# Feed-forward values in PSUM, offsets by two ScalarE passes, and GpSimd's scale products by position in the block

## The chip, the cores and the metric

The kernel runs on one core of one Trainium2 chip. The metric is the device time of one execution in microseconds (us); lower is better. The kernel before takes 913.84 us, the median of three runs (913.34 to 918.64).

Five engines work side by side, each with its own instruction stream: TensorE (PE), VectorE (DVE), ScalarE (ACT), GpSimd (POOL) and SyncE (SP, which here only issues DMAs). They wait for each other through semaphores. Each stream runs in the order in which it was written: an instruction whose semaphore isn't there yet holds up all that stand behind it on its engine.

## The reference

The input is x, 2 x 2048 rows of 128 values. Four residual steps follow each other: a landmark attention, a feed-forward, a linear attention, and the same feed-forward once more. The change touches the two feed-forward steps alone. In short:

```python
def fp4_quant_dequant(x):                      # blocks of 16 along the row
    scale = max(max|xb| / 6, 1e-12)
    xn = xb / scale
    idx = searchsorted(_MID, |xn|)             # nearest of 0 .5 1 1.5 2 3 4 6
    return _GRID[idx] * sign(xn) * scale

h = silu(q(x) @ q(w_gate).T) * (q(x) @ q(w_up).T)      # q is fp4_quant_dequant
y = q(h) @ q(w_down).T                                  # x: 128, h: 352 values a row
x = x + ffn(layernorm(x))
```

So each row's normalised x (128 values, 8 blocks) and each row's h (352 values, 22 blocks) is rounded to an eight-value grid with one scale for each block of 16.

## The kernel before, in words

The 4096 rows are 32 **tiles** of 128 rows (one row a partition). x is quantised by the **quad** (four tiles, 512 values a partition, q = 0 to 7), h by the **pair** (two tiles, 704 values a partition, r = 0 to 15). The function ffn(p) stands once in each engine's stream for each of the two feed-forward stages, p = 0 and p = 1.

**How a value is rounded.** DVE takes the largest magnitude of each block (absmax, L818). POOL makes the scale from it (L248), DVE its reciprocal (L823) and the ratio value/scale (ratio_of, L828). ACT writes an offset, the magnitude times 2^22, in bf16 (absolute, L557), DVE clamps that from below (offset_of, L834) and adds it to the ratio (move_by, L838). This addition rounds the ratio to its grid. POOL subtracts the offset again (L255 for x, L265 for h) and multiplies by the scales (L258, L268); there each scale is repeated 16 times by a step of zero. All of these tiles lie in SBUF.

**The rest of a pair.** PE transposes the four tiles of a quad (L1180), ACT copies them to SBUF (L534). For each tile PE makes gate and up (gate_up, L1188 and L1189) into two PSUM banks, ACT takes silu of the gate (L540), DVE multiplies it by up (gated, L845) into h. The rounded h is transposed by PE (L1197, six transposes a pair), copied by ACT (L546), multiplied by w_down on PE (L1206, twelve weight loads), copied by ACT (L552) and added to X by POOL (L273). In p = 0 DVE also takes statistics of finished tiles (L648, L650), and POOL makes the layernorm constants (L320). In p = 1 SP stores each finished quad (L234).

**The order.** Every engine's stream is a loop written out over r from -4 to 18, with q = (r + 4) // 2. Quads are worked on while q < 8, so up to r = 11: absmax, scale and ratio of a quad in the even iteration, the addition, POOL's passes, the transposes and the copy in the odd one. In iteration r:

- DVE: gated(2r), gated(2r+1), absmax of h, x part, reciprocal and ratio of h, x part, offset and addition of h.
- POOL: the scales of x (even r) and of pair r, the two passes of pair r-1, in odd r the two passes of quad q, the residual of pair r-3.
- PE: gate_up(2r+2), down of pair r-2, gate_up(2r+3), in odd r the transposes of quad q, the transposes of pair r-1.
- ACT: copy of pair r-2's transposes, silu(2r+2), down copy of pair r-2, silu(2r+3), offset of h for pair r, in even r that of x, in odd r normalise(q+1) (L526: four instructions, the layernorm of the next quad) and last the copy of quad q's transposes.

PSUM has eight banks. Banks 0 to 3 hold gate and up of two tiles, 4 and 5 the transposes of h, 6 those of x, 7 the down product. The functions that the change touches and what calls them:

## Time and profile before

| | |
|---|---|
| three runs, median | 913.84 us (913.34 to 918.64) |
| the profiled execution, its own time | 913.45 us |
| its span, first to last instruction | 911.7 us |
| mean granted TensorE clock | 0.85 |
| busy share: PE, PE weight loads | 70%, 51% |
| busy share: DVE, ACT, POOL | 64%, 33%, 39% |
| first feed-forward stage | about 383 to 547 us |
| second feed-forward stage | about 745 us to the end |

PE's row counts matmuls, PEld its weight loads, which overlap. A busy share is an average over stages with different limits, and idle time of an engine that is not the limit costs nothing; what bounds a stage is read from who waits for whom in it. The "chain of waits" follows the work back from its last instruction, at each step to what released it. The granted clock is the share of full speed that TensorE was given.

### The profile page before, as it was taken

The numbers are of one execution on the slowest core, as the hardware profiler recorded it, in microseconds if no ns is written. First come the engines' busy times: TensorE is split into PE (matmuls) and PEld (weight loads), VectorE is DVE, ScalarE is ACT, GpSimd is POOL, SyncE is SP. The second block draws the span as 40 slices with busy tenths as digits, with TensorE's granted clock in tenths as the row PEclk, the third lists the DMA queues.
The fourth block names the chain that finished last, engine by engine and source line by source line (L and its number), as shares of the span: only waits on it lengthen the run. The fifth ranks groups of instructions, "written<-read, shape, count | busy, mean of one in ns | idle before, by whom it ended". The sixth has DMA issues, their size and how long they took to land.

```text
span 911.7 us, 14036 instructions
## 1 busy us (share of the span) xinstructions
PE 639.3 (70%) x5231; PEld 464.9 (51%) x5231; DVE 584.0 (64%) x1062; ACT 300.4 (33%) x507; POOL 354.6 (39%) x423
## 2 busy tenths in 40 slices
...
DMA packets 13676, 10.47 MB, mean 11 GB/s; under 512 B 1399, under 2 KB 12599, under 8 KB 13493
## 3 DMA queue, kind: packets, MB, share of 16 engines
...
q14 instruction: 21, 0.16, 0.1%
...
## 4 chain that ended last, share of the span: by engine, by line
PE 48%; DVE 23%; POOL 13%; issue 10%; ACT 5%; ACTq 0%; DMA 0%; DVEq 0%; POOLq 0%
PE ps L1052 5%; PE ps L1138 4%; PE ps L1270 4%; PE ps L1206 3%; PE ps L1167 3%; PE ps L1079 3%; PE ps L1188 3%; POOL arena L268 3%; PE ps L1289 2%; POOL arena L265 2%; DVE r L770 2%; POOL arena L258 2%; PE ps L1197 2%; DVE arena L845 2%; DVE hblk L818 2%
## 5 line engine op out<-in xcount | busy, mean ns | idle before, releaser
L1188 PE MATMUL ps<-wguT,arena 128*128 128x352 f32 x128 | 61.9, 572 | 34.5 <-DVE arena L845 33.1
L320 POOL TENSOR_TENSOR ln<-mv,lnc 128x4 f32<-128x4 f32 x64 | 13.6, 213 | 154.7 <-DVE mv L650 154.7
L339 POOL MEMSET early<- 128x2560 f32 x2 | 4.5, 2231 | 172.3 <-PE ps L1123 161.6
L1138 PE MATMUL ps<-G,xw 128*126 128x512 f32 x72 | 46.6, 800 | 30.0 <-ACT xw L492 22.3
L1180 PE MATMUL ps<-eye,arena 128*128 128x128 f32 x64 | 15.3, 383 | 73.7 <-POOL arena L258 65.3
L368 POOL TENSOR_SCALAR_AFFINE_SELECT arena<-arena 128x1024 f32<-128x1024 f32 x32 | 35.0, 1093 | 80.6 <-ACT arena L607 80.6
L1206 PEld LDWEIGHTS ps<-wdT,arena 128*128 128x128 f32 (+1 forms) x384 | 57.7, 226 | 15.2 <-ACT arena L546 7.6
L1206 PE MATMUL ps<-wdT,arena 128*128 128x128 f32 (+1 forms) x384 | 58.4, 311 | 5.4 <-ACT arena L546 5.4
L268 POOL TENSOR_TENSOR arena<-arena,hblk 128x704 f32<-128x704 f32 x32 | 60.1, 1880 | 2.5
L1189 PE MATMUL ps<-wguT,arena 128*128 128x352 f32 x128 | 57.1, 532 | 0.0
L931 DVE TENSOR_TENSOR arena<-ps,tri 128x1024 f32<-128x1024 f32 x32 | 39.2, 1224 | 27.2 <-PE ps L1270 27.2
L828 DVE SCALAR_TENSOR_TENSOR arena<-arena,hblk 128x704 f32<-128x704 f32 x32 | 53.3, 1665 | 3.3
L1180 PEld LDWEIGHTS ps<-eye,arena 128*128 128x128 f32 x64 | 9.7, 186 | 82.3 <-POOL arena L258 64.2
L607 ACT ACTIVATE arena<-ps 128x1024 f32<-128x1024 f32 x32 | 32.8, 1025 | 53.7 <-PE ps L1270 53.7
L265 POOL TENSOR_TENSOR arena<-arena,hoff 128x704 f32<-128x704 f32 x32 | 48.6, 1519 | 4.1 <-PE ps L1197 1.6
L1188 PEld LDWEIGHTS ps<-wguT,arena 128*128 128x128 f32 x128 | 24.7, 233 | 42.1 <-issue 39.3
L1197 PE MATMUL ps<-eye,arena 128*128 128x128 f32 (+1 forms) x192 | 37.2, 348 | 12.2 <-POOL arena L268 12.2
L1148 PEld LDWEIGHTS ps<-band,A 126*32 126x32 f32 x1152 | 32.3, 122 | 24.4 <-DVE A L795 20.9
L1148 PE MATMUL ps<-band,A 126*32 126x114 f32 x1152 | 35.5, 287 | 13.0 <-DVE A L795 13.0
L540 ACT ACTIVATE arena<-ps 128x352 f32<-128x352 f32 x64 | 29.6, 463 | 43.1 <-PE ps L1188 42.9
L1052 PE MATMUL ps<-arena 128*128 128x128 f32 x288 | 37.4, 289 | 8.9 <-DVE arena L734 7.2
L770 DVE TENSOR_REDUCE r<-ps 126x48 f32<-126x1536 f32 x12 | 21.1, 1755 | 33.7 <-PE ps L1138 33.7
...
## 6 DMA issues: line engine op xcount, KB each, us to landing
...
```

What stands on the lines that cost most here:

```text
L265: tt(out=hgrid, in0=hmoved[k], in1=hoff[k][:, :], op=ALU.subtract).then_inc(s["fh_grid"], 1)
L268: tt(out=blocks(hquant[k].rearrange("p k n -> p (k n)")), in0=blocks(hgrid), in1=hblk[k][:, 2, :].unsqueeze(2).broadcast_to([P, 2 * F // B ...
L770: reduce(out=r1[:, 0, :], in_=psf[0:WI, 0:NW * HM].rearrange("p (k m) -> p k m", m=M), axis=AX, op=ALU.max).then_inc(s["s1_max"], 1)
L828: stt(out=rat.rearrange("p (k j) -> p k j", j=BLK), in0=src.rearrange("p (k j) -> p k j", j=BLK), scalar=TIE, in1=b[:, 1, :].unsqueeze(2). ...
L931: tt(out=masked[n % 2][:, 0:8, :], in0=psf[:, 0:2 * QW].rearrange("p (h t) -> p h t", t=P), in1=tri[:, :].unsqueeze(1).broadcast_to([P, 8, ...
L1052: last = mm(banks(bank + hf, 1, P)[:, u, :], lhsT[:, 4 * hf + u, :], rhs[:, 4 * hf + u, :], start=True, stop=True)
L1138: last = mm(ps[0:WI, w, :], xw[:, w * WO:w * WO + WI], G1[:, b, :], start=True, stop=True)
L1148: last = mm(ps[32 * c:32 * c + 32, 4 + g, w * WO:(w + 1) * WO], A1v[:, w, h * M:(h + 1) * M], band[:, h, :], start=True, stop=True)
L1188: mm(ps[:, 2 * k, 0:F], x, wguT[:, 0:F], start=True, stop=True).then_inc(s["f_gate"], 1)
L1189: mm(ps[:, 2 * k + 1, 0:F], x, wguT[:, F:2 * F], start=True, stop=True).then_inc(s["f_up"], 1)
L1197: last = tp(ps[0:FK[c], 4 + k, c * P:(c + 1) * P], hquant[r % 2][:, k, c * P:c * P + FK[c]], eye[:, :])
L1206: last = mm(ps[:, 7, k * P:(k + 1) * P], hT[r % 2][0:FK[c], k, c, :], wdT[0:FK[c], c, :], start=(c == 0), stop=(c == 2))
```

## The change

- The normalised x is written by ACT into PSUM bank 7; maximum, ratio (in place) and addition read it there. The gated product is written over the up values in PSUM (banks 1 and 2, or 3 and 4, by the pair's parity), and h's maximum, ratio (in place) and addition work there.
- All gates share bank 0. The transposes of x and of h's first tile share bank 5; those of h's second tile and the down product share bank 6. The waits follow from that.
- The offset is no longer Abs on ACT and a clamp on DVE, but Square on ACT, a wait, and Identity with a constant bias on ACT, both bf16.
- POOL's scale products walk by position in the block: for each of 16 positions all blocks in turn, so that in0 and the output step by 16 values (64 bytes) and the scales are read one after the other.
- The copy of h's transposes is two instructions, one a tile.
- On PE and ACT, the transposes of quad q and their copy now stand between the first and the second tile's gate/up and silu of an odd iteration. normalise(q+1) stays where it was, which is now behind that copy.
- In p = 1 DVE adds the down product to X straight from PSUM; ACT's down copy and POOL's residual are left out there. In p = 1 ACT waits for the end of the linear attention before normalise(0).

The core of the diff, without most of the removed lines, which the listing above has, and with indentation taken off; the parts are, in order, GpSimd, ScalarE, VectorE and TensorE:

```diff
+GATE_BANK, X_BANK, T_BANK = 0, 7, 5
+SQ = (RND / 6.0) ** 0.5
...
+def up_banks(r):
+    return ps[:, 1 + 2 * (r % 2):3 + 2 * (r % 2), 0:F]
+def columns(t):
+    return t.rearrange("p (k j) -> p j k", j=BLK)
...
-    tt(out=blocks(xquant.rearrange("p k c -> p (k c)")), in0=blocks(xgrid),
-       in1=xblk[:, 2, :].unsqueeze(2).broadcast_to([P, QD * P // BLK, BLK]), op=ALU.mult).then_inc(s["fx_quant"], 1)
+    tt(out=columns(xquant.rearrange("p k c -> p (k c)")), in0=columns(xgrid),
+       in1=xblk[:, 2, :].unsqueeze(1).broadcast_to([P, BLK, QD * P // BLK]), op=ALU.mult).then_inc(s["fx_quant"], 1)
...
-    tt(out=blocks(hquant[k].rearrange("p k n -> p (k n)")), in0=blocks(hgrid),
-       in1=hblk[k][:, 2, :].unsqueeze(2).broadcast_to([P, 2 * F // BLK, BLK]), op=ALU.mult).then_inc(s["fh_quant"], 1)
+    tt(out=columns(hquant[k].rearrange("p k n -> p (k n)")), in0=columns(hgrid),
+       in1=hblk[k][:, 2, :].unsqueeze(1).broadcast_to([P, BLK, 2 * F // BLK]), op=ALU.mult).then_inc(s["fh_quant"], 1)
...
-    if 0 <= r - 3 < PN:
+    if p == 0 and 0 <= r - 3 < PN:
         residual(r - 3)
...
     a.wait_ge(s["moment_step"], (p + p + 1) * TILES + (q + 1) * QD)
-    need(a, "fx_ratio", n)
+    need(a, "fx_moved", n)
...
-        last = act(xin[:, k * P:(k + 1) * P], X[:, t, :], ACT.Identity, scale=rstd[:, t:t + 1],
+        last = act(ps[:, X_BANK, k * P:(k + 1) * P], X[:, t, :], ACT.Identity, scale=rstd[:, t:t + 1],
...
+    act(xT[q % 2], ps[:, T_BANK, :].rearrange("p (k c) -> p k c", k=QD), ACT.Copy).then_inc(s["fx_T_copied"], 1)
+    act(sil[t % 2], ps[:, GATE_BANK, 0:F], ACT.Silu).then_inc(s["f_silu"], 1)
...
     need(a, "f_down", n - 1)
+    for k in range(2):
+        a.wait_ge(s["fh_T"], 2 * n + k + 1)
+        act(hT[r % 2][:, k, :, :], ps[:, T_BANK + k, 0:3 * P].rearrange("p (c n) -> p c n", c=3),
+            ACT.Copy).then_inc(s["fh_T_copied"], 1)
 def down_copy(r):
     n = ffn_pairs(p, r)
     a.wait_ge(s["f_down"], n + 1)
     need(a, "f_x_done", n - 1)
+    act(down[r % 2], ps[:, T_BANK + 1, 0:2 * P].rearrange("p (k c) -> p k c", k=2), ACT.Copy).then_inc(s["f_down_copied"], 1)
+def offset_x(q):
+    n = ffn_quads(p, q)
+    a.wait_ge(s["fx_ratio"], n + 1)
+    need(a, "fx_offset", n)
+    act(xsquare[:, :], ps[:, X_BANK, :], ACT.Square, scale=SQ).then_inc(s["fx_square"], 1)
+    a.wait_ge(s["fx_square"], n + 1)
+    need(a, "fx_grid", n)
+    act(xoff[:, :], xsquare[:, :], ACT.Identity, bias=lnc[:, 3:4]).then_inc(s["fx_offset"], 1)
+def offset_h(r):
+    n = ffn_pairs(p, r)
+    a.wait_ge(s["fh_ratio"], n + 1)
+    need(a, "fh_offset", n)
+    act(hsquare[:, :].rearrange("p (k n) -> p k n", k=2), up_banks(r), ACT.Square, scale=SQ).then_inc(s["fh_square"], 1)
+    a.wait_ge(s["fh_square"], n + 1)
+    need(a, "fh_grid", n - 1)
+    act(hoff[r % 2][:, :], hsquare[:, :], ACT.Identity, bias=lnc[:, 3:4]).then_inc(s["fh_offset"], 1)
+if p == 1:
+    a.wait_ge(s["lin_x_done"], TILES)
 normalise(0)
 for r in range(-FILL, PN + 3):
     q = (r + FILL) // 2
...
         hT_copy(r - 2)
     if 0 <= r + 1 < PN:
         silu(2 * r + 2)
-    if 0 <= r - 2 < PN:
+    if 0 <= r - 2 < PN and p == 0:
         down_copy(r - 2)
+    if r % 2 and q < QN:
+        xT_copy(q)
     if 0 <= r + 1 < PN:
         silu(2 * r + 3)
     if 0 <= r < PN:
-        absolute("fh", hratio, hoff[r % 2], ffn_pairs(p, r), ffn_pairs(p, r) - 1)
+        offset_h(r)
     if r % 2 == 0 and q < QN:
-        absolute("fx", xratio, xoff, ffn_quads(p, q), ffn_quads(p, q))
+        offset_x(q)
     if r % 2 and q + 1 < QN:
         normalise(q + 1)
-    if r % 2 and q < QN:
-        xT_copy(q)
...
+def x_blocks():
+    return ps[:, X_BANK:X_BANK + 1, :]
+def absmax_x(q):
+    n = ffn_quads(p, q)
+    v.wait_ge(s["fx_norm"], n + 1)
+    reduce(out=xblk[:, 0, :].unsqueeze(1), in_=blocks(x_blocks()), axis=AX, op=ALU.max,
+           apply_absolute_value=True).then_inc(s["fx_absmax"], 1)
+def ratio_x(q):
+    n = ffn_quads(p, q)
+    inverse("fx", xblk, n)
+    v.wait_ge(s["fx_inverse"], n + 1)
+    stt(out=blocks(x_blocks()), in0=blocks(x_blocks()), scalar=TIE,
+        in1=xblk[:, 1, :].unsqueeze(1).unsqueeze(3).broadcast_to([P, 1, QD * P // BLK, BLK]), op0=ALU.mult,
+        op1=ALU.mult).then_inc(s["fx_ratio"], 1)
+def move_x(q):
+    n = ffn_quads(p, q)
+    v.wait_ge(s["fx_offset"], n + 1)
+    need(v, "fx_grid", n)
+    tt(out=xmoved, in0=ps[:, X_BANK, :], in1=xoff[:, :], op=ALU.add).then_inc(s["fx_moved"], 1)
 def gated(t):
     n = ffn_tiles(p, t)
     v.wait_ge(s["f_silu"], n + 1)
     v.wait_ge(s["f_up"], n + 1)
+    up = up_banks(t // 2)[:, t % 2, :]
+    tt(out=up, in0=up, in1=sil[t % 2], op=ALU.mult).then_inc(s["f_h"], 1)
+def absmax_h(r):
+    v.wait_ge(s["f_h"], ffn_tiles(p, 2 * r + 2))
+    reduce(out=pair(hblk[r % 2][:, 0, :]), in_=blocks(up_banks(r)), axis=AX, op=ALU.max,
+           apply_absolute_value=True).then_inc(s["fh_absmax"], 1)
+def ratio_h(r):
+    n = ffn_pairs(p, r)
+    v.wait_ge(s["fh_inverse"], n + 1)
+    stt(out=blocks(up_banks(r)), in0=blocks(up_banks(r)), scalar=TIE,
+        in1=pair(hblk[r % 2][:, 1, :]).unsqueeze(3).broadcast_to([P, 2, F // BLK, BLK]), op0=ALU.mult,
+        op1=ALU.mult).then_inc(s["fh_ratio"], 1)
+def move_h(r):
+    n = ffn_pairs(p, r)
+    v.wait_ge(s["fh_offset"], n + 1)
+    need(v, "fh_grid", n - 1)
+    tt(out=pair(hmoved[r % 2]), in0=up_banks(r), in1=pair(hoff[r % 2][:, :]), op=ALU.add).then_inc(s["fh_moved"], 1)
+def residual(r):
+    v.wait_ge(s["f_down"], ffn_pairs(p, r + 1))
+    tt(out=X[:, 2 * r:2 * r + 2, :], in0=ps[:, T_BANK + 1, 0:2 * P].rearrange("p (k c) -> p k c", k=2),
+       in1=X[:, 2 * r:2 * r + 2, :], op=ALU.add).then_inc(s["f_x_done"], 1)
+for r in range(-FILL, PN + (4 if p == 0 else 3)):
     q = (r + FILL) // 2
+    if 0 <= r < PN:
         gated(2 * r)
         gated(2 * r + 1)
+        absmax_h(r)
+    if r % 2 == 0 and q < QN:
+        absmax_x(q)
+    if r % 2 and q < QN:
+        move_x(q)
+    if p == 1 and 0 <= r - 2 < PN:
+        residual(r - 2)
+    if 0 <= r < PN:
+        inverse("fh", hblk[r % 2], ffn_pairs(p, r))
+        ratio_h(r)
+    if r % 2 == 0 and q < QN:
+        ratio_x(q)
     if p == 0 and 0 <= r - 4 < PN:
         v.wait_ge(s["f_x_done"], ffn_pairs(p, r - 3))
         tile_stats(2, 2 * r - 8)
         tile_stats(2, 2 * r - 7)
+    if 0 <= r < PN:
+        move_h(r)
 ffn(0)
...
+def x_transposes(q, r):
     n = ffn_quads(p, q)
     pe.wait_ge(s["fx_quant"], n + 1)
+    need(pe, "fh_T_copied", 2 * ffn_pairs(p, min(max(r - 1, 0), PN)))
     for k in range(QD):
+        last = tp(ps[:, T_BANK, k * P:(k + 1) * P], xquant[:, k, :], eye[:, :])
     last.then_inc(s["fx_T"], 1)
 def gate_up(t):
+    n, r = ffn_tiles(p, t), t // 2
     pe.wait_ge(s["fx_T_copied"], ffn_quads(p, t // QD + 1))
+    need(pe, "f_silu", n)
     x = xT[t // QD % 2][:, t % QD, :]
+    mm(ps[:, GATE_BANK, 0:F], x, wguT[:, 0:F], start=True, stop=True).then_inc(s["f_gate"], 1)
+    need(pe, "fh_moved", ffn_pairs(p, max(r - 1, 0)))
+    mm(up_banks(r)[:, t % 2, :], x, wguT[:, F:2 * F], start=True, stop=True).then_inc(s["f_up"], 1)
 def h_transposes(r):
     n = ffn_pairs(p, r)
     pe.wait_ge(s["fh_quant"], n + 1)
+    need(pe, "fx_T_copied", ffn_quads(p, min((r + 1 + FILL + 1) // 2, QN)))
+    need(pe, "fh_T_copied", 2 * n)
+    for k in range(2):
+        if k == 1:
+            need(pe, "f_x_done" if p else "f_down_copied", n)
+        for c in range(3):
+            last = tp(ps[0:FK[c], T_BANK + k, c * P:(c + 1) * P], hquant[r % 2][:, k, c * P:c * P + FK[c]], eye[:, :])
+        last.then_inc(s["fh_T"], 1)
+def down_mms(r):
+    n = ffn_pairs(p, r)
+    pe.wait_ge(s["fh_T_copied"], 2 * n + 2)
     for k in range(2):
         for c in range(3):
+            last = mm(ps[:, T_BANK + 1, k * P:(k + 1) * P], hT[r % 2][0:FK[c], k, c, :], wdT[0:FK[c], c, :],
                       start=(c == 0), stop=(c == 2))
     last.then_inc(s["f_down"], 1)
...
         gate_up(2 * r + 2)
     if 0 <= r - 2 < PN:
         down_mms(r - 2)
+    if r % 2 and q < QN:
+        x_transposes(q, r)
     if 0 <= r + 1 < PN:
         gate_up(2 * r + 3)
-    if r % 2 and q < QN:
-        x_transposes(q)
     if 0 <= r - 1 < PN:
         h_transposes(r - 1)
```

## Rows read from the trace of the kernel before

**Rows 1.** Windows: length, busy us of PE, PEld, DVE, ACT, POOL (instructions), clock, DMA.
```profile
403.70:513.70 110.00, 70.93 (x324) 52.98 (x324) 94.65 (x148) 47.09 (x90) 78.82 (x79) 0.85 0.00 1
...
765.75:875.77 110.02, 70.85 (x324) 53.04 (x324) 90.08 (x112) 47.09 (x90) 72.37 (x63) 0.85 0.04 13
```

**Rows 2.** Chain of waits, second stage: start us, length us, what (xcount).
```profile
779.41 1.34 PE ps L1206 x12
...
784.72 0.90 DVE hblk L818
...
786.20 1.52 POOL arena L265
...
787.80 1.91 POOL arena L268
...
790.34 1.19 POOL arena L255
...
791.60 1.59 POOL arena L258
...
793.24 1.12 PE ps L1180 x4
...
795.64 1.17 PE ps L1188 x2
...
800.97 0.79 ACT hoff L557
```

**Rows 3.** Timeline of DVE: start us, us, engine, line, operation, output<-inputs, xcount.
```profile
782.93 0.89 DVE L838 TENSOR_TENSOR arena<-arena,hoff 128x704 f32<-128x704 f32 x1
...
783.74 0.94 DVE L845 TENSOR_TENSOR arena<-arena,ps 128x352 f32<-128x352 f32 x2
...
786.68 1.79 DVE L828 SCALAR_TENSOR_TENSOR arena<-arena,hblk 128x704 f32<-128x704 f32 x1
...
792.20 0.94 DVE L845 TENSOR_TENSOR arena<-arena,ps 128x352 f32<-128x352 f32 x2
...
795.60 0.43 DVE L823 RECIPROCAL hblk<-hblk 128x44 f32<-128x44 f32 x1 [0.95 <-POOL hblk L248]
```

**Rows 4.** Timeline of POOL beside an idle DVE, same columns.
```profile
389.52 1.06 POOL L258 TENSOR_TENSOR arena<-arena,xblk 128x512 f32<-128x512 f32 x1
...
900.43 1.38 POOL L268 TENSOR_TENSOR arena<-arena,hblk 128x704 f32<-128x704 f32 x1
```

**Rows 5.** Groups by line and shape: busy us, mean ns | idle before, releaser.
```profile
L540 ACT ACTIVATE arena<-ps 128x352 f32<-128x352 f32 x64 | 29.6, 463 | 43.1 <-PE ps L1188 42.9
...
L546 ACT ACTIVATE arena<-ps 128x768 f32<-128x768 f32 x32 | 25.8, 807 | 18.6 <-PE ps L1197 18.2
...
L534 ACT ACTIVATE arena<-ps 128x512 f32<-128x512 f32 x16 | 9.5, 595 | 50.2 <-PE ps L1180 50.2
...
L588 ACT ACTIVATE arena<-ps,bias_qk 128x512 f32<-128x512 f32 x8 | 5.5, 687 | 1.8 <-PE ps L1236 1.8
...
L363 POOL TENSOR_TENSOR arena<-arena 128x512 f32<-128x512 f32 x8 | 10.1, 1263 | 8.1 <-DVE arena L898 8.1
...
L885 DVE SCALAR_TENSOR_TENSOR arena<-ps,bias_qk,arena 128x512 f32<-128x512 f32 x8 | 6.0, 751 | 19.3 <-POOL arena L358 19.3
...
L770 DVE TENSOR_REDUCE r<-ps 126x48 f32<-126x1536 f32 x12 | 21.1, 1755 | 33.7 <-PE ps L1138 33.7
```

**Rows 6.** Timeline at the start and the end of the second stage.
```profile
747.17 0.33 POOL L248 TENSOR_SCALAR xblk<-xblk 128x32 f32<-128x32 f32 x1
...
749.26 1.63 ACT L526 ACTIVATE arena<-X,ln 128x128 f32<-128x128 f32 x4
...
875.77 0.94 DVE L845 TENSOR_TENSOR arena<-arena,ps 128x352 f32<-128x352 f32 x2
...
891.26 0.95 DVE L845 TENSOR_TENSOR arena<-arena,ps 128x352 f32<-128x352 f32 x2
...
908.26 0.72 POOL L273 TENSOR_TENSOR X<-X,arena 128x256 f32<-128x256 f32 x1 [4.38 <-ACT arena L552]
```

More of the change, by code:

```diff
@@ L81, in build @@
         ln = sb("ln", [P, 4, TILES])
-        lnc = sb("lnc", [P, 3])
+        lnc = sb("lnc", [P, 4])
         rstd, shift = ln[:, 1, :], ln[:, 3, :]
@@ L102, in build @@
         used[0] = 0
-        xin, xratio, xmoved, xgrid = (part(QD * P) for _ in range(4))
+        xmoved, xgrid = (part(QD * P) for _ in range(2))
         xquant = part(QD * P).rearrange("p (k c) -> p k c", k=QD)
@@ L106, in build @@
         sil = [part(F) for _ in range(2)]
-        h, hratio, hgrid = (part(2 * F) for _ in range(3))
+        hgrid = part(2 * F)
         hmoved = [part(2 * F) for _ in range(2)]
@@ L297, in _ @@
                 g.memset(XNT[:, b, HALO + N:NPAD], 0.0)
-            for k, c in enumerate((1e-5, -0.5, -1.0)):
+            for k, c in enumerate((1e-5, -0.5, -1.0, RND * 4.0 / 3.0)):
                 g.memset(lnc[:, k:k + 1], c)
@@ L533, in xT_copy @@
                     need(a, "f_up", ffn_tiles(p, (q - 1) * QD))
-                    act(xT[q % 2], ps[:, 6, :].rearrange("p (k c) -> p k c", k=QD), ACT.Copy).then_inc(s["fx_T_copied"], 1)
+                    act(xT[q % 2], ps[:, T_BANK, :].rearrange("p (k c) -> p k c", k=QD), ACT.Copy).then_inc(s["fx_T_copied"], 1)
                 def silu(t):
@@ L551, in down_copy @@
                     need(a, "f_x_done", n - 1)
-                    act(down[r % 2], ps[:, 7, 0:2 * P].rearrange("p (k c) -> p k c", k=2), ACT.Copy).then_inc(s["f_down_copied"], 1)
-                def absolute(name, rat, off, n, freed):
-                    a.wait_ge(s[name + "_ratio"], n + 1)
-                    need(a, name + "_grid", freed)
-                    act(off[:, :], rat, ACT.Abs, scale=RND).then_inc(s[name + "_abs"], 1)
+                    act(down[r % 2], ps[:, T_BANK + 1, 0:2 * P].rearrange("p (k c) -> p k c", k=2), ACT.Copy).then_inc(s["f_down_copied"], 1)
[17 more added lines that the diff above has]
+                    a.wait_ge(s["lin_x_done"], TILES)
                 normalise(0)
@@ L816, in ffn, with pair, blocks @@
             def ffn(p):
-                def absmax(name, src, b):
-                    reduce(out=b[:, 0, :], in_=src.rearrange("p (k j) -> p k j", j=BLK), axis=AX, op=ALU.max,
-                           apply_absolute_value=True).then_inc(s[name + "_absmax"], 1)
+                def pair(t):
+                    return t.rearrange("p (k n) -> p k n", k=2)
+                def blocks(t):
+                    return t.rearrange("p k (b j) -> p k b j", j=BLK)
                 def inverse(name, b, n):
@@ L823, in inverse @@
                     recip(out=b[:, 1, :], in_=b[:, 2, :]).then_inc(s[name + "_inverse"], 1)
-                def ratio_of(name, src, rat, b, n):
-                    v.wait_ge(s[name + "_inverse"], n + 1)
-                    nb = b.shape[2]
-                    stt(out=rat.rearrange("p (k j) -> p k j", j=BLK), in0=src.rearrange("p (k j) -> p k j", j=BLK), scalar=TIE,
-                        in1=b[:, 1, :].unsqueeze(2).broadcast_to([P, nb, BLK]), op0=ALU.mult,
-                        op1=ALU.mult).then_inc(s[name + "_ratio"], 1)
-                def offset_of(name, off, n):
-                    v.wait_ge(s[name + "_abs"], n + 1)
-                    ts(out=off[:, :], in0=off[:, :], scalar1=RND_MIN, scalar2=None, op0=ALU.max).then_inc(s[name + "_offset"], 1)
-                def move_by(name, rat, off, mov, n):
-                    v.wait_ge(s[name + "_offset"], n + 1)
-                    tt(out=mov, in0=rat, in1=off[:, :], op=ALU.add).then_inc(s[name + "_moved"], 1)
+                def x_blocks():
[17 more added lines that the diff above has]
+                    tt(out=xmoved, in0=ps[:, X_BANK, :], in1=xoff[:, :], op=ALU.add).then_inc(s["fx_moved"], 1)
                 def gated(t):
@@ L843, in gated @@
                     v.wait_ge(s["f_up"], n + 1)
-                    need(v, "fh_ratio", ffn_pairs(p, t // 2))
-                    tt(out=h[:, (t % 2) * F:(t % 2 + 1) * F], in0=sil[t % 2], in1=ps[:, 2 * (t % 2) + 1, 0:F],
-                       op=ALU.mult).then_inc(s["f_h"], 1)
-                for r in range(-FILL, PN + (4 if p == 0 else 0)):
+                    up = up_banks(t // 2)[:, t % 2, :]
[4 more added lines that the diff above has]
+                           apply_absolute_value=True).then_inc(s["fh_absmax"], 1)
@@ L852, in ffn @@
-                    if hh:
+                    if 0 <= r < PN:
                         gated(2 * r)
                         gated(2 * r + 1)
-                        v.wait_ge(s["f_h"], ffn_tiles(p, 2 * r + 2))
-                        absmax("fh", h, hblk[k])
-                    if x and k == 0:
-                        v.wait_ge(s["fx_norm"], nq + 1)
-                        absmax("fx", xin, xblk)
-                    if x and k == 1:
-                        offset_of("fx", xoff, nq)
+                        absmax_h(r)
@@ L865, in ffn @@
                         tile_stats(2, 2 * r - 7)
-                    if hh:
-                        inverse("fh", hblk[k], n)
-                        need(v, "fh_moved", n)
-                        ratio_of("fh", h, hratio, hblk[k], n)
-                    if x and k == 0:
-                        inverse("fx", xblk, nq)
-                        need(v, "fx_moved", nq)
-                        ratio_of("fx", xin, xratio, xblk, nq)
-                    if x and k == 1:
-                        move_by("fx", xratio, xoff, xmoved, nq)
-                    if hh:
-                        offset_of("fh", hoff[k], n)
-                        move_by("fh", hratio, hoff[k], hmoved[k], n)
+                    if 0 <= r < PN:
+                        move_h(r)
             ffn(0)
```

23 lines of the change are left out of this document (1 added, 22 removed).

## The prediction

> **What bounds the kernel now.** I read the windows first, then the chain of waits, then the timeline. The change lies in the two feed-forward stages alone. In each, the twelve row pairs from r = 1 to 12, in which new rows are still being quantised beside the pairs, take 110.0 us, 18.34 us per odd and even iteration, with DVE busy 82 to 86% [rows 1]. The chain of one such round [rows 2] shows what the page's sum does not: it starts with DVE's maximum in an odd iteration, goes through four POOL passes in a row (L265, L268, L255, L258), the x transposes, a gate/up, a down product and another gate/up, and comes back to DVE through ACT's L557 in the even iteration. DVE is nearly as full, so both matter.
>
> DVE's fullness is partly waiting. The ratio L828 takes 1.79 us when POOL is at work, the add L838 0.89 when it is not [rows 3], for the same 704 elements. L268 takes 1.91 us in the chain [rows 2] and 1.38 at 900.43, L258 1.59 against 1.06 at 389.52 [rows 4], DVE being idle there. In the timeline a stretched DVE pass ends about one plain duration after POOL's pass ends, so the two engines take turns. The gated product, one operand in PSUM, is not stretched: two take 0.94 us [rows 3].
>
> **The change, part by part.** Time 0 is the start of the gated products of an odd iteration, 783.74 in the trace. Handoffs are those of the rows: 0.04 us, 0.07 between POOL passes; DVE's next product starts 0.81 after its last add (782.93 to 783.74) [rows 3].
>
> *Removed.* Every DVE pass with two SBUF streams goes to PSUM, so I take the turns as gone: POOL 1.38 and 1.06 as in [rows 4], DVE unstretched. DVE's clamp (0.3 us) and, in the second stage, ACT's down copy and POOL's residual go; DVE does that residual. From L770 (1536 elements, 1.755) and the maximum (704, 0.90) [rows 2, 5] DVE takes 1.04 ns an element over 0.16 us, so 0.42 for 256.
>
> *Added on ACT.* One Abs (0.79, L557 [rows 2]) becomes Square, a wait on it, then Identity. L534 (512, 595 ns) and L546 (768, 807 ns) give 0.755 for 704 from PSUM. Identity is 0.79 plus a pointer bias: L588 against L534 prices it 0.09 [rows 5]. With 0.08 for the wait, the pair is 1.71, for x 1.39 (0.60, 0.08, 0.71). ACT wide over a wait has no nearer row; bounds 1.6 to 1.9.
>
> *POOL's scale products* (in0 and output now step 64 bytes, in1 is contiguous). At 512 elements the trace has 1.06 with a repeated in1 [rows 4], 1.19 with a bf16 in1 [rows 2], 1.26 with a contiguous fp32 in1 (L363 [rows 5]): 0.2 us for four more bytes an element. If a stepped fp32 read costs like twice its bytes, that is 0.2 once more: 1.47 for x, and for h 1.38 + 2 x 0.28 = 1.94. Bounds: no effect (1.06 and 1.38), and writes paying too (1.67 and 2.22). I take the middle, since both the new in1 and the new step are seen or implied by those rows.
>
> The Trainium skill (GPSIMD Engine Reference, section Performance pitfalls for Q7 kernels) speaks against this edit: a read stepping more than 8 bytes costs 2.9 cycles an element instead of 1.9. As an estimate, one cycle more at its 1.2 GHz makes 1.49 and 1.97, and the sum would be 1 us higher; no row shows a stepped read.
>
> *Moved: the order on PE and ACT.* This decides. In an odd iteration r, PE now transposes quad q before gate/up of tile 2r+3, and ACT copies it before silu of 2r+3; behind that silu stand the two offset passes of pair r, for which DVE's last add of the same iteration waits. But POOL gives quad q only after pair r's maximum, its scales, and both passes of pair r-1. So POOL's four passes are now inside DVE's own iteration, where before the transposes stood behind that gate/up and ACT's copy stood last. What this adds queues up everything behind: the add, the next products, POOL's next pass.
>
> Odd iteration: POOL's L265 starts at 2.46 [rows 2, 3] and ends 3.98; L268 4.05 to 5.99; L255 6.06 to 7.25; L258 7.32 to 8.79. Transposes 8.85 to 9.97 (1.12), gate half 1.17 to 11.15 [rows 2], PE being slow after a pause of over 5 us; silu 0.46 (L540 [rows 5]) to 11.65; offset to 13.41; the add and handoff 0.85: 14.26, against 8.46 before.
>
> Even iteration: the reciprocal starts 3.40 after the first product (792.20 to 795.60), the ratio 0.53 later [rows 3] (from POOL's scales, unchanged): 18.19, ends 19.14 with 0.95 as in the next paragraph. Offset 20.90, add 21.75. In the second stage ACT's normalise (1.60) runs to 15.0, the split hT copy 0.95 to 15.95, down 1.5 (1.34 in [rows 2], slower at times) to 17.5, DVE's new residual to 17.95, so the ratio is 0.35 later: 22.1. Mean round 21.9. Six are 131.5; r = 12 has no x work, -1.25. Against 110.0: +20.2 per stage.
>
> DVE on PSUM: the stt L885 with a PSUM input takes 0.751 us for 512, 0.06 over the 0.69 of 1.04 ns an element; L770, a reduce from PSUM, fits the same line as an SBUF one [rows 5]. I charge 0.06 on the ratio alone. The Trainium skill (VectorE: DVE Perf Modes, section The TRN2 errata) has a fixed 120 cycles for a PSUM source against 58 for SBUF; as an estimate, six passes on the path a round would then pay 0.065 each and the sum would be 4 us higher. Half the rows agree. Writes of DVE into PSUM are in no row: bounded by 0 and 0.3 us a round, taken as 0.
>
> Start of each stage, from POOL's scale at 747.17 [rows 6]: X's single bank makes normalise(1) wait for the first add, and ACT's new order puts it behind xT_copy(0), so behind POOL's first two passes. Scale, reciprocal and ratio to 748.75; offset 750.18; add 750.91; POOL 753.68; transposes and copy 755.48; normalise (1.63 [rows 6]) 757.1; maximum, scale, ratio 759.55; offset and add 761.7; POOL 764.5; transposes, gate/up(1) 768.0; product, maxima, scales, ratio 772.5; offset and add 775.1, where 765.75 stood: +9.3. ACT waiting for the end of the attention costs nothing, as POOL's moments end later still.
>
> Pairs 13 and 14 took 15.5 us (875.77 to 891.26 [rows 6]); without turns the recurrence (product and maximum 1.88, scales 0.54, reciprocal 0.53, ratio 0.95, offset 1.75, add 0.85, residual part 0.3) is 6.8, call it 7.0 for a slow PE: -1.5. The drain saves the down copy and most of POOL's 0.72 [rows 6] in the second stage: -1.1; -0.4 in the first.
>
> Sum: 2 x (9.3 + 20.2 - 1.5) - 1.5 = +54.5. The profiled execution took 913.45 us (span 911.7), 0.4 under the median 913.84. **Forecast 968 us.**
>
> **Rivals.**
> *A, faster.* The turns between DVE and POOL set the round, and the new order is covered. Then the round is DVE's own: even 3.40 + 0.53 + 0.95 + 1.76 + 0.85 = 7.49; odd 1.88 + 0.69 (x add) + 0.42 + 0.53 + 0.95 + 1.75 + 0.85 = 7.07. Of 18.34, 14.56 stay, and 12 x 3.78 = 45 us go: 868. For it: DVE at 82 to 86%. Against: the chain runs through POOL. It decides at the first odd iteration: only if the x transposes were ready before silu(2r+3) would ask, at about 3.2 us, while POOL's four passes alone end at 8.8. Chance 4%.
> *B, the step is free for POOL* (1.38 and 1.06): 0.97 a round and as much at the start: 968 - 13 = 955. Chance 20%.
> *C, writes pay too* (2.22, 1.67): +0.48 a round, +1 at the starts: 975. 13%.
> *D, the slow clock reaches further.* With PE pausing over 5 us a round, down and gate/up in the even iteration run at 1.2 GHz too: +1.2 a round, 982. For it: mean clock 0.85 now with shorter pauses [rows 1]. 13%.
> *E, PSUM operands don't end the turns*, so the change doesn't do what it says: POOL pays 0.53 twice in the odd iteration: 981. Against: the unstretched product. 4%.
> *F, partial hiding*: the starts cost half and PE is fast at once (-0.8 a round): 968 - 19 = 949; 10%. Something smaller still, within 1% of before: 3%.
> The forecast itself has 33%.
>
> **Numbers.** Range: B and F at the low end with part of each other, 944; D with the upper offset bound at the high end, 987. About 1% is what a measurement of this kernel tells from no change: slower by more than that 0.93 (all but A and the last), same 0.03, faster 0.04.
>
> **What would show it.** DVE idle for some 9 us (8 with the statistics of the first stage) in front of h's last add in odd iterations, and about 1 to 2 in even ones; rounds near 22 us; the transposes waiting for POOL and silu for them; POOL's h product at 1.9 and x at 1.5, never stretched; DVE's ratio at 0.95; DVE's share down, and the granted clock below 0.85. I am wrong if rounds are under 19 us, if DVE's add follows the ratio within 2 us in odd iterations, or if ratio passes still take 1.8.

## The result, and the profile after

The changed kernel takes 961.74 us, the median of four runs (960.36 to 966.51), against 914.25 us (913.34 to 918.64): 1.052 times the time before, 95% interval 1.048 to 1.056. The profiled execution took 962.55 us. I had forecast 968 us, 944 to 987.

The page of the changed kernel, and its windows over iterations 1 to 12 of both stages (columns as in [rows 1]):

```profile
span 960.8 us, 14051 instructions
...
PE 663.7 (69%) x5231; PEld 472.9 (49%) x5231; DVE 517.9 (54%) x1030; ACT 334.0 (35%) x571; POOL 343.2 (36%) x408
...
L899 DVE TENSOR_TENSOR arena<-ps,hoff 128x704 f32<-128x704 f32 x32 | 28.5, 892 | 111.7 <-ACT hoff L582 111.7
```

```profile
414.35:540.62 126.27, 76.81 (x318) 53.96 (x319) 65.30 (x130) 60.78 (x118) 75.20 (x75) 0.80 0.00 1
798.26:925.13 126.87, 78.88 (x318) 55.27 (x319) 62.68 (x106) 56.41 (x107) 64.17 (x53) 0.77 0.04 11
```

DVE fell from 584.0 to 517.9 us of work (64 to 54% of the span) while the kernel grew: its stretched passes and its clamps are gone. The granted clock fell from 0.85 to 0.84. L899, the last add of h, heads the list not for its work but for 111.7 us of waiting for ACT. The windows, which answer to [rows 1], took 110.0 and now take 126.3 and 126.9 us: 21.05 and 21.15 us a round against 18.34.

The chain of one round of the second stage (as [rows 2]) and DVE's timeline over it (as [rows 3]):

```profile
820.66 0.90 DVE hblk L885
822.15 1.52 POOL arena L275
...
825.70 1.18 POOL arena L265
826.94 1.53 POOL arena L268
828.51 1.11 PE ps L1230 x4
829.63 1.17 PE ps L1238 x2
...
832.77 1.51 ACT ps L536 x4
835.20 1.62 PE ps L1259 x12
837.64 0.91 DVE ps L891
839.36 0.89 ACT hoff L582
```

```profile
819.67 0.95 DVE L881 TENSOR_TENSOR ps<-ps,arena 128x352 f32<-128x352 f32 x2
...
823.67 0.90 DVE L891 SCALAR_TENSOR_TENSOR ps<-ps,hblk 128x704 f32<-128x704 f32 x1
832.90 0.89 DVE L899 TENSOR_TENSOR arena<-ps,hoff 128x704 f32<-128x704 f32 x1 [8.32 <-ACT hoff L582]
833.70 0.95 DVE L881 TENSOR_TENSOR ps<-ps,arena 128x352 f32<-128x352 f32 x2
...
840.27 0.89 DVE L899 TENSOR_TENSOR arena<-ps,hoff 128x704 f32<-128x704 f32 x1 [0.75 <-ACT hoff L582]
```

From 819.67 to 833.70 the odd iteration takes 14.03 us; the even one, which ends with the next product at 841.08, takes 7.38. The chain is the forecast one: DVE's maximum, POOL's L275 and L278 (2.02 us from 823.74, of which the chain shows most as a gap), L265, L268, the x transposes, the gate half, then ACT; normalise and down lead through DVE's residual (836.85, not shown) to the even iteration's ratio. DVE stands idle for 8.32 us in front of L899 in the odd iteration and 0.75 in the even one, and the ratio takes 0.90 us beside a busy POOL, where it took 1.79 [rows 3].

Groups by line that answer to [rows 5] and [rows 4], the start of the second stage (as [rows 6]), and its end:

```profile
L278 POOL TENSOR_TENSOR arena<-arena,hblk 128x704 f32<-128x704 f32 x32 | 65.0, 2032 | 2.5
...
L268 POOL TENSOR_TENSOR arena<-arena,xblk 128x512 f32<-128x512 f32 x16 | 24.3, 1519 | 1.3
...
L582 ACT ACTIVATE hoff<-hsquare,lnc 128x704 bf16<-128x704 bf16 x32 | 28.2, 882 | 1.0
...
L579 ACT ACTIVATE hsquare<-ps 128x704 bf16<-128x704 f32 x32 | 24.1, 755 | 16.4 <-DVE ps L891 16.4
...
L881 DVE TENSOR_TENSOR ps<-ps,arena 128x352 f32<-128x352 f32 x64 | 30.8, 524 | 11.8 <-PE ps L1240 9.7 <-ACT arena L550 2.2
L891 DVE SCALAR_TENSOR_TENSOR ps<-ps,hblk 128x704 f32<-128x704 f32 x32 | 28.8, 899 | 1.1
```

```profile
770.77 0.33 POOL L258 TENSOR_SCALAR xblk<-xblk 128x32 f32<-128x32 f32 x1 [0.18 <-DVE xblk L859]
...
778.89 1.60 ACT L536 ACTIVATE ps<-X,ln 128x128 f32<-128x128 f32 x4
```

```profile
940.38 0.95 DVE L881 TENSOR_TENSOR ps<-ps,arena 128x352 f32<-128x352 f32 x2
...
957.64 0.42 DVE L903 TENSOR_TENSOR X<-ps,X 128x256 f32<-128x256 f32 x1 [5.58 <-PE ps L1259]
```

POOL's products take 2.03 and 1.52 us where they took 1.38 and 1.06 undisturbed [rows 4]; Square and Identity 0.755 and 0.882; the gated product and the ratio write PSUM at 0.52 and 0.90 us, as they wrote SBUF. From POOL's scale at 770.77 to iteration 1 at 798.26 go 27.5 us, against 18.6 [rows 6]. After iteration 15's products (940.38) 20.4 us are left, against 20.4 from 891.26 [rows 6].

| stretch (profiled executions, us) | before | after | difference | forecast |
|---|---|---|---|---|
| up to the first stage's iteration 1 | 403.7 | 414.4 | +10.7 (1.7 of it ahead of the stage) | +9.3 |
| iterations 1 to 12, first stage | 110.1 | 126.3 | +16.2 | +20.2 |
| from 13 to the first scan of the attention | 45.6 | 42.1 | -3.5 | -1.9 |
| linear attention | 185.1 | 185.2 | +0.1 | 0 |
| start of the second stage | 21.3 | 30.3 | +9.0 | +9.3 |
| iterations 1 to 12, second stage | 110.0 | 126.9 | +16.9 | +20.2 |
| from 13 to the end | 35.9 | 35.7 | -0.3 | -2.6 |

### The profile page after: what moved, and what is told of

It reads as the page before. It is cut to its first block, busy times and chain, and to the rows that moved or that the text cites. A ratio compares the mean times of both kernels' runs of the same rounds, so it can differ in the third digit from the quotient of the medians.

```text
span 960.8 us, 14051 instructions
## 1 busy us (share of the span) xinstructions
PE 663.7 (69%) x5231; PEld 472.9 (49%) x5231; DVE 517.9 (54%) x1030; ACT 334.0 (35%) x571; POOL 343.2 (36%) x408
## 4 chain that ended last, share of the span: by engine, by line
PE 42%; DVE 23%; POOL 12%; issue 12%; ACT 9%; POOLq 0%; ACTq 0%; DMA 0%; DVEq 0%
PE ps L1102 5%; PE ps L1188 4%; PE ps L1322 4%; PE ps L1217 3%; PE ps L1129 3%; POOL arena L275 3%; POOL arena L268 2%; PE ps L1341 2%; DVE ps L881 2%; DVE hblk L885 2%; DVE r L796 2%; ACT hoff L582 2%; PE ps L1259 2%; POOL arena L265 2%; ACT hsquare L579 2%
## 5 line engine op out<-in xcount | busy, mean ns | idle before, releaser
L899 DVE TENSOR_TENSOR arena<-ps,hoff 128x704 f32<-128x704 f32 x32 | 28.5, 892 | 111.7 <-ACT hoff L582 111.7
L1251 PE MATMUL ps<-eye,arena 128*128 128x128 f32 (+1 forms) x192 | 40.1, 367 | 46.2 <-POOL arena L278 46.2
L1240 PE MATMUL ps<-wguT,arena 128*128 128x352 f32 x128 | 64.3, 592 | 9.9 <-DVE arena L899 9.8
L1238 PE MATMUL ps<-wguT,arena 128*128 128x352 f32 x128 | 66.2, 608 | 1.7 <-ACT arena L544 1.4
L278 POOL TENSOR_TENSOR arena<-arena,hblk 128x704 f32<-128x704 f32 x32 | 65.0, 2032 | 2.5
L1251 PEld LDWEIGHTS ps<-eye,arena 128*128 128x128 f32 (+1 forms) x192 | 31.3, 186 | 63.6 <-POOL arena L278 56.1
L275 POOL TENSOR_TENSOR arena<-arena,hoff 128x704 f32<-128x704 f32 x32 | 48.6, 1517 | 4.8 <-DVE arena L899 2.4
L1240 PEld LDWEIGHTS ps<-wguT,arena 128*128 128x128 f32 x128 | 31.2, 251 | 35.3 <-DVE arena L899 17.7
L1198 PEld LDWEIGHTS ps<-band,A 126*32 126x32 f32 x1152 | 32.1, 122 | 24.6 <-DVE A L821 21.1
L507 ACT ACTIVATE S<-S 126x512 f32<-126x512 f32 x36 | 21.9, 629 | 61.9 <-DVE S L804 61.9
```

The costliest lines, as they stand in the source:

```text
L275: tt(out=hgrid, in0=hmoved[k], in1=hoff[k][:, :], op=ALU.subtract).then_inc(s["fh_grid"], 1)
L278: tt(out=columns(hquant[k].rearrange("p k n -> p (k n)")), in0=columns(hgrid), in1=hblk[k][:, 2, :].unsqueeze(1).broadcast_to([P, BLK, 2 * ...
L1198: last = mm(ps[32 * c:32 * c + 32, 4 + g, w * WO:(w + 1) * WO], A1v[:, w, h * M:(h + 1) * M], band[:, h, :], start=True, stop=True)
L1238: mm(ps[:, GATE_BANK, 0:F], x, wguT[:, 0:F], start=True, stop=True).then_inc(s["f_gate"], 1)
L1240: mm(up_banks(r)[:, t % 2, :], x, wguT[:, F:2 * F], start=True, stop=True).then_inc(s["f_up"], 1)
L1251: last = tp(ps[0:FK[c], T_BANK + k, c * P:(c + 1) * P], hquant[r % 2][:, k, c * P:c * P + FK[c]], eye[:, :])
```

## The experiments

Theory 1 is the prediction's: the new order of the x transposes and their copy puts POOL's four passes inside DVE's own iteration. Theory 2: the shared PSUM banks and their waits cost the time. Theory 3: POOL's stepped products do. All were run beside the kernel before, whose median lay between 914.5 and 915.2 us. A round is a mean over iterations 1 to 12 of both stages of the profiled execution; "(one)" marks a kernel that ran once.

| kernel | time, us | ratio to before (95%) | round, us |
|---|---|---|---|
| before | 914.3 | 1 | 18.34 |
| changed | 961.7 | 1.048 to 1.056 | 21.1 |
| e1, changed, order of before | 937.6 | 1.022 to 1.031 | 20.3 |
| e2, changed, only PE's order of before | 953.6 (one) | - | 20.9 |
| e3, changed, only ACT's order of before | 988.5 (one) | - | 24.0 |
| e4, changed, repeated scales | 937.9 | 1.020 to 1.036 | 20.1 |
| e10, changed, order and scales of before | 914.3 | 0.998 to 1.003 | 18.6 |
| e5, before, products by position | 935.0 | 1.020 to 1.025 | 19.9 |
| e6, before, new order | 970.3 | 1.059 to 1.064 | 22.3 |
| e7, changed, Abs and clamp | 959.7 | 1.046 to 1.051 | 21.5 |
| e8, third order, repeated scales | 903.2 | 0.983 to 0.991 | 17.8 |
| e9, offset first, repeated scales | 870.8 | 0.950 to 0.959 | 15.1 |
| e12, e9 with products by position | 877.1 | 0.955 to 0.968 | 15.7 |
| e11, before, order of e9 | 900.1 | 0.981 to 0.990 | 17.4 |

**e1, the order put back.**

```diff
 # PE
+    gate_up(2 * r + 3)
     if r % 2 and q < QN:
         x_transposes(q, r)
-    gate_up(2 * r + 3)
 # ACT: xT_copy(q) from before silu(2 * r + 3) to behind normalise(q + 1)
```

> The changed kernel with the order of before on PE and ACT: the x transposes behind gate/up(2r+3), their copy last in ACT's iteration. Theory 1 (the order puts POOL's four passes inside DVE's own iteration): odd iterations fall from 14.0 us to DVE's own 7.1, but the copy of the x transposes now stands in front of h's transposes (shared bank), so the round is POOL 8.9, transposes 1.1, copy 0.6, h's transposes 1.3, copy 0.9, down 1.5, gate and silu 1.2, offsets 1.7, add 0.85, about 18.2 against 21.4; 12 rounds and the starts give about 914 us (905 to 925). Theory 2 (the new waits come from the shared banks: one gate bank, one bank for both transposes): no gain, 955 to 965. Theory 3 (POOL's stepped product is the loss): no gain either.

It took 937.6: 24 us came back, half of what was expected. Odd iterations fell, to 6.3 us in the first stage (7.1 had been expected) and to between 6.3 and 8.2 in the second; even ones grew to between 12.3 and 14.9. The timeline of one of the first stage shows why, with one line of the second stage at the end:

```profile
455.13 0.60 ACT L544 ACTIVATE arena<-ps 128x512 f32<-128x512 f32 x1 [2.96 <-PE ps L1230]
...
455.82 1.51 PE L1251 MATMUL ps<-eye,arena 128*128 128x128 f32 x6 [0.73 <-issue]
...
457.13 1.38 PE L1238 MATMUL ps<-wguT,arena 128*128 128x352 f32 x2
...
459.48 2.22 PE L1259 MATMUL ps<-wdT,arena 128*128 128x128 f32 x12
...
464.39 0.89 DVE L899 TENSOR_TENSOR arena<-ps,hoff 128x704 f32<-128x704 f32 x1 [5.71 <-ACT hoff L582]
...
833.93 0.42 DVE L903 TENSOR_TENSOR X<-ps,X 128x256 f32<-128x256 f32 x1 [6.25 <-PE ps L1259]
```

h's transposes (455.82) wait for the copy of the x transposes (455.13) in the bank that they now share, and then a whole gate/up at the slow clock (457.13 on; 1.38 us for a gate that takes 0.76 at full speed) and a down of 2.2 us stand in front of the silu that the offset waits for. My sum for this kernel had left out that gate/up. In the second stage the same chain reaches DVE one step earlier: the residual, new on DVE there (L903), stands in front of the reciprocal and waits for that down product, 6.25 us at 833.93, and the add then waits only 0.75 us. So theory 2 has a part too: in the order of before, the shared bank and the longer products together make the round 20.3, not 18.2.

**e2 and e3, one engine's order put back.** Of e1's edit, e2 has PE's half, e3 ACT's.

> Only PE's order put back: gate/up(2r+3) ahead of the x transposes, ACT still copies them ahead of silu(2r+3). Theory 1: silu still waits for the copy, only the gate half drops out of the chain, 0.55 us a round less, about 954 us. If PE's order alone were the cause: near 914.

> Only ACT's order put back, PE still transposes x ahead of gate/up(2r+3). Theory 1: silu(2r+3) still waits for that gate, so odd iterations stay at 14.0, and h's transposes wait for a copy that now stands behind the offsets and normalise: some 1.5 us a round more, but a faster start (5 us a stage): 965 to 975 us. If ACT's order alone were the cause: near 914.

e2 came out where theory 1 put it, 953.6. e3 is worse than expected, 988.5 against 965 to 975: the direction is the theory's, the size isn't. Its odd iterations stay at 14.0 us, as expected, but its even ones take 9.8 in the first stage and 9.4 to 11.8 in the second, against 7.4. I had counted only the wait for the copy; behind it come a gate/up at the slow clock (1.30 and 1.38 us at 451.69 and 452.78) and the down, and in the second stage DVE's residual waits for that down:

```profile
849.46 0.42 DVE L903 TENSOR_TENSOR X<-ps,X 128x256 f32<-128x256 f32 x1 [3.79 <-PE ps L1259]
```

Neither half alone gives e1's gain, so silu(2r+3) is held from both sides.

**e4, repeated scales.**

```diff
-    tt(out=columns(hquant ...), in0=columns(hgrid), in1=... .unsqueeze(1).broadcast_to([P, BLK, 2 * F // BLK]) ...)
+    tt(out=blocks(hquant ...), in0=blocks(hgrid), in1=... .unsqueeze(2).broadcast_to([P, 2 * F // BLK, BLK]) ...)
     # and the same for x
```

> The changed kernel with POOL's scale products walked block by block with repeated scales, as before. Theory 1: the products take 1.38 and 1.06 us in place of 2.03 and 1.52, both on the chain of a round: 12 x 1.11 + 2 for the starts + 1 for the drains, so 946 us. If POOL still took turns with DVE they would take 1.9 and 1.6 and nothing would change (960). If the walk by position were no dearer: 961.

POOL's products went to 1.384 and 1.057 us, the round fell by 1.0, as expected, but the kernel by 24 us, not 16. In the profiled executions 12.4 of them lie in the two windows, 1.8 in the starts, 3.8 behind iteration 12, and 6 in the linear attention, whose instructions are the same. Windows over it, e4's first and then the changed kernel's:

```profile
574.90:754.00 179.10, 153.96 (x1704) 97.86 (x1704) 117.56 (x242) 64.26 (x101) 90.15 (x116) 0.92 0.01 2
```

```profile
582.70:767.90 185.20, 163.26 (x1707) 103.04 (x1705) 117.58 (x241) 64.37 (x101) 90.20 (x116) 0.86 0.01 2
```

PE was granted 0.92 of its clock in e4 and 0.86 in the changed kernel, in the first 20.6 us of the stretch 0.75 against 0.50. Why, the runs don't say. It is also one execution of each: e4's profiled one took 938.5 us at a mean clock of 0.87, two others 936.2 and 937.3 at 0.84. Over all profiled executions of this document the attention takes 179.1 to 185.4 us, so a difference of 6 us or less between two kernels can't be put down to the feed-forward stages without looking there.

**e10, order and scales of before,** the move to PSUM, the two ACT passes and DVE's residual alone.

> The changed kernel with both the order and POOL's repeated scales of before: what is left of the change is the values in PSUM, the shared banks, the two ACT passes and DVE's residual. Theory 1: against the run with only the order put back (937.6) the two products give back 1.11 us a round and 3 at the ends, or the 24 us that they gave back in the new order: 914 to 921 us, so the PSUM move alone is worth nothing against the kernel before: what it gains in turns it gives to the copy of x's transposes that now stands in front of h's, and to the longer offset. If the move alone were a gain: below 905.

914.3 against 915.2 us, ratio 0.998 to 1.003: in sum the first half of the change does nothing for the time. The sum hides parts that go both ways. The window over iterations 1 to 12 is 108.0 us in the first stage, 2.1 less than before, and 115.2 in the second, 5.2 more; there DVE waits at its residual:

```profile
797.43 0.42 DVE L903 TENSOR_TENSOR X<-ps,X 128x256 f32<-128x256 f32 x1 [4.76 <-PE ps L1259]
```

No run puts the residual back on POOL by itself, so what it costs isn't shown. From here, the new order adds 24 us (e4) and the walk by position 23 (e1); together they make the 47. With the attention left out of the profiled executions, the order adds 23 to 28 us and the walk 18 to 22.

**e5 and e6, one part alone on the kernel before.** e5 has e4's edit the other way round, e6 the new order on PE and ACT.

> The kernel before with nothing but POOL's two scale products walked by position. Theory 1: they take 2.03 and 1.52 us plus the wait for DVE's turn (0.53 each), so 2.5 and 2.0 on a chain of 18.3 us that holds both in odd iterations: up to +1.1 a round plus the starts, and DVE waits longer for its turns: 925 to 935 us. If the walk cost nothing: 914.

> The kernel before with nothing but the new order on PE and ACT (x transposes and their copy between the two gate/up and silu). Theory 1: POOL's last pass ends 9.5 us after the first product, then transposes 1.1, gate 1.2, silu 0.5, Abs 0.8, clamp and add 1.2: odd iterations 14.3 us, even ones about 9: 23.3 against 18.3, so 12 x 5 plus 10 for the starts: about 980 us (965 to 990). Theory 2 (shared banks): 914 to 925, for here the banks are apart.

e5, 935.0, came out at the upper end of its range, e6, 970.3, inside. POOL's products in e5 (groups by line):

```profile
L271 POOL TENSOR_TENSOR arena<-arena,hblk 128x704 f32<-128x704 f32 x32 | 81.1, 2534 | 2.5
...
L261 POOL TENSOR_TENSOR arena<-arena,xblk 128x512 f32<-128x512 f32 x16 | 30.8, 1924 | 1.3
```

2.53 and 1.92 us: for h 0.65 us over 1.38 for the step, as in the changed kernel, and 0.50 more for the wait for DVE's turn. DVE's timeline of a round in e6:

```profile
476.61 0.95 DVE L845 TENSOR_TENSOR arena<-arena,ps 128x352 f32<-128x352 f32 x2
...
489.07 0.34 DVE L834 TENSOR_SCALAR hoff<-hoff 128x704 bf16<-128x704 bf16 x1 [5.92 <-ACT hoff L557]
...
490.25 0.95 DVE L845 TENSOR_TENSOR arena<-arena,ps 128x352 f32<-128x352 f32 x2
```

Odd iterations take 13.6 us, with DVE waiting 5.9 us for L557: with the banks of before, the new order alone costs 55 us. It costs 24 in the new layout (e10 to e4). Put the other way, the new layout is worth 32 us in the new order (e6 to e4) and nothing in the order of before (before to e10). So the order is shown to be enough by itself, and theory 2 alone is not.

**e7, the offset as before.**

```diff
-    act(hsquare, up_banks(r), ACT.Square, scale=SQ); wait; act(hoff, hsquare, ACT.Identity, bias=lnc[:, 3:4])
+    act(hoff, up_banks(r), ACT.Abs, scale=RND)                                   # ACT
+    ts(out=hoff, in0=hoff, scalar1=RND_MIN, op0=ALU.max); wait                   # DVE, ahead of the add
```

> The changed kernel with the offset made as before: Abs on ACT from PSUM (0.76) and the clamp on DVE (0.34). On the path stand 0.76 + 0.04 + 0.38 in place of 0.76 + 0.03 + 0.88, so 0.45 us less in each of the 32 pairs and some in the x chains of the starts: about 946 us. If the clamp has to wait for POOL's pass it gains less or nothing in even iterations (it was 0.59 in place of 0.34 before): 950 to 955. If ACT's passes were covered: 961.

959.7 where about 946 had been expected: 2 us less than the changed kernel, too little to tell from none. The timeline, even iteration first:

```profile
453.12 2.04 POOL L278 TENSOR_TENSOR arena<-arena,hblk 128x704 f32<-128x704 f32 x1
...
454.55 0.82 DVE L896 TENSOR_SCALAR hoff<-hoff 128x704 bf16<-128x704 bf16 x1
...
468.52 0.35 DVE L896 TENSOR_SCALAR hoff<-hoff 128x704 bf16<-128x704 bf16 x1 [7.44 <-ACT hoff L578]
```

In the odd iteration the clamp takes 0.35 us and the iteration is 0.5 shorter. In the even one it ends 0.2 us after POOL's L278 does (455.16) and takes 0.82; the even iteration is 0.8 longer. In the second stage the clamp of an even iteration takes 1.62 us, and again ends 0.2 after L278. The second ACT pass is long, but it never waits for POOL: 0.88 us in all 32 pairs.

**e8, a third order.**

```diff
 # PE, iteration r
     gate_up(2r+2); gate_up(2r+3); h_transposes(r-1); x_transposes(q); down_mms(r-1)
 # ACT, iteration r
     silu(2r+2); down_copy(r-2); silu(2r+3); offset_h(r); offset_x(q) or normalise(q+1); hT_copy(r-1); xT_copy(q)
 # PE's two waits for the shared bank follow the new order; POOL's products as in e4
```

> The changed kernel with repeated scales and a third order: both gate/up of an iteration first, then h's transposes of pair r-1, x's transposes, down of pair r-1; on ACT both silu, offsets, normalise, and last the two copies of transposes. Theory 1: nothing of the quad stands between silu(2r+3) and the gate, so DVE's own round (odd 7.1, even 7.5, POOL's scales in front of the even reciprocal) of 14.6 to 15.5 us is left, against 21.4: 12 x 6 + 10 for starts + 8 for POOL's shorter products where they still count: 865 to 885 us, which would beat both kernels. Theory 2 (shared banks bind): 930 to 950.

903.2: faster than both kernels, but not the 865 to 885 that were expected. Its timeline shows what is left:

```profile
448.58 1.38 PE L1238 MATMUL ps<-wguT,arena 128*128 128x352 f32 x2
...
450.00 0.46 ACT L550 ACTIVATE arena<-ps 128x352 f32<-128x352 f32 x1 [3.65 <-PE ps L1238]
...
451.85 0.75 ACT L579 ACTIVATE hsquare<-ps 128x704 bf16<-128x704 f32 x1
...
453.55 0.89 DVE L899 TENSOR_TENSOR arena<-ps,hoff 128x704 f32<-128x704 f32 x1 [3.75 <-ACT hoff L582]
```

The gate of 448.58 runs at the slow clock, its silu ends at 450.46, the second gate and silu follow, and only then Square (451.85). DVE waits 3.75 us for it.

**e9, the offset first.**

```diff
 # ACT, iteration r, against e8
+    offset_h(r)
     silu(2 * r + 3)
-    offset_h(r)
     offset_x(q)
+    hT_copy(r - 1)
     normalise(q + 1)
-    hT_copy(r - 1)
```

> The third order once more, with ACT's two offset passes of pair r ahead of silu(2r+3) instead of behind it, and the copy of h's transposes ahead of normalise. In the third order's trace DVE still waits 2.5 to 3.8 us before each last add, because silu(2r+3) waits for a gate at the slow clock and the offsets stand behind it. Theory 1 (a round is set by what stands in ACT's stream in front of the offsets): these waits fall to 1.7 and 0.8 us, rounds from 17.7 to about 15, so 12 x 2.5 off 903: 870 to 880 us. If PE's own work at the slow clock binds the round instead (about 17 us of it), 895 to 905.

870.8 us, 0.950 to 0.959 of the time before. DVE's last adds of an even and an odd iteration:

```profile
803.30 0.89 DVE L899 TENSOR_TENSOR arena<-ps,hoff 128x704 f32<-128x704 f32 x1 [0.75 <-ACT hoff L582]
...
812.06 0.89 DVE L899 TENSOR_TENSOR arena<-ps,hoff 128x704 f32<-128x704 f32 x1 [1.74 <-ACT hoff L582]
```

The waits are 0.75 and 1.74 us, the 0.8 and 1.7 that were named: here what is left in front of the add is ACT's own two passes. In the second stage that holds for every iteration; in the first the odd ones wait 1.5 to 2.8. Yet the first stage's window takes 87.7 us and the second's 93.7, where DVE's residual waits too:

```profile
808.63 0.42 DVE L903 TENSOR_TENSOR X<-ps,X 128x256 f32<-128x256 f32 x1 [2.05 <-PE ps L1259]
```

**e11 and e12: what the move to PSUM and the walk are worth in this order.**

> The kernel before, all values in SBUF, with the order of the fastest run (offset ahead of silu(2r+3), transposes and down at the end of the iteration). It tells what the move to PSUM is worth once the order no longer hides it. If the turns between DVE and POOL cost what the trace of before says: odd iterations stay at DVE's stretched 8.5 us, even ones fall from 9.9 to about 8.7, so 17.2 a round against 18.34, 12 x 1.15 off: about 900 us (893 to 908). If the turns cost nothing and the order alone made the gain: 870 to 880.

> The fastest order with POOL's products walked by position again (2.03 and 1.52 us in place of 1.38 and 1.06). Where these stood on the chain they cost 24 us. Here POOL's passes of an odd iteration end near 9 us and its next scales are asked for at 9.7, so little is on the path: 873 to 880 us. If POOL's passes are still on the chain: 12 x 1.11 + 4 more, 888.

Both as expected. With the order of e9 the layout of before stops at 900.1 us and the PSUM layout reaches 870.8: the first half of the change, which ends the turns between DVE and POOL, is worth 29 us once the order lets it show. That counts the two ACT passes and DVE's residual with it; how much is the end of the turns alone isn't separated. The walk by position costs 6 us there, and 20 to 24 on the chains of before and of the change (e5, e1, e4).

## Why the prediction was right

**The order.** The step "POOL's four passes are now inside DVE's own iteration" held to the instruction: 14.03 us measured against 14.26 for the odd iteration, DVE's wait 8.3 against "some 9". In the second stage's later odd iterations (5 to 11) the wait in front of the add is only 5.2 to 6.7 us, because DVE already waits 2.2 to 3.6 at its residual for the down product; that wait is covered there, and these iterations take 13.4 to 14.05 us all the same. e6 shows it alone, e1 to e3 that both engines' halves are needed. The even iteration took 7.38, against 7.49 and, with the residual, 7.84: down and DVE's residual ended beside POOL's scales and cost nothing (within 0.1 us; the ratio starts 3.94 us after the first product, where 4.28 was the forecast with them). In the second stage six such rounds, each 0.2 and 0.46 us shorter than forecast, make 4 us, about the size by which its window came out lower than my rounds of 22.1 give. In the first stage, with no residual on DVE, rounds of 21.75 less 1.25 make 129.3, and it took 126.3: 2.3 of the 3 us lie in the odd iterations, most of them in one of 13.19 and one of 13.67 us, where the x transposes took 0.66 us and not 1.12. PE was already at its high clock there, a part of rival F.

**The starts.** +9.0 against +9.3, for the reasons given: normalise(1) stands at 778.89, behind the copy.

**POOL's products.** 2.03 and 1.52 us against 1.94 and 1.47. The estimate of 1.97 and 1.49 by the Trainium skill (GPSIMD Engine Reference, section Performance pitfalls for Q7 kernels) was the nearer. Measured are 0.65 us more for 704 elements and 0.46 for 512, 0.9 ns each; whether the step of in0, that of the output or the scales read one after the other costs it, no run separates. The mis-sized term is what this does to the whole: I had rival B, no effect of the step, 13 us below the forecast; taking the step away gave 24 us. The rounds were priced well, 12.4 us for 11.6. Left out were the ends (3.8) and the attention (6, at a higher clock, which no price of the walk could foresee). I had also put most of the loss on the order. The runs divide it in about halves: 24 and 23. So that the total came out within 7 us is in part luck: the walk cost more than I gave it, the rest less.

**Turns and PSUM.** DVE was never stretched again, and rival E is out. The ratio took 0.90 us against 0.95 forecast; the Trainium skill (VectorE: DVE Perf Modes, section The TRN2 errata) has a fixed 120 cycles for a PSUM source against 58, and this doesn't show here: the maximum takes 0.89 us from SBUF and from PSUM.

**The drain.** -2.6 forecast, -0.3 measured in the second stage. Of the -1.5 for pairs 13 and 14 came -0.2, of the -1.1 behind them nothing. The term that I had wrong is DVE's new residual: I had given it 0.3 us, but it stands in front of the reciprocal and waits for its down product. It did so for 2.52 us in iteration 13 (of 8.64 us, where 14 took 6.61) and again in iteration 15. The first two lines are of the changed kernel, the last two of the one before:

```profile
941.50 2.93 PE L1259 MATMUL ps<-wdT,arena 128*128 128x128 f32 x12 [0.69 <-ACT arena L557]
...
944.47 0.42 DVE L903 TENSOR_TENSOR X<-ps,X 128x256 f32<-128x256 f32 x1 [2.21 <-PE ps L1259]
...
891.01 1.60 PE L1206 MATMUL ps<-wdT,arena 128*128 128x128 f32 x12 [0.90 <-ACT arena L546]
...
894.21 1.77 DVE L828 SCALAR_TENSOR_TENSOR arena<-arena,hblk 128x704 f32<-128x704 f32 x1
```

PE ran at half its clock for the first of these (granted 0.50) and at full clock for the one of before. The ratio starts 4.9 us after the product there (945.27 from 940.38), against 2.95 before, and that eats what the down copy and the stretched passes give back. POOL's longer product isn't the cause: from L275 to PE's transposes of the last pair go 3.7 us, against 3.6 before. e4 ends this stretch 3.6 us sooner, but there a down takes 1.60 us at the full clock in front of the residual, and another at the very end.

Rival A, the faster side, asked that nothing of the quad stand before silu(2r+3). e9 meets that with repeated scales, e12 with all of the change but its order; they take 870.8 and 877.1 us, close to the 868 that it was given, in rounds of 15.1 and 15.7 us for 14.6. Its price was nearly right, its condition wasn't met by the change.

What stays open: why the attention is granted more or less clock from kernel to kernel, and what DVE's residual in the second stage costs by itself.
